# One hand-written schedule of a decoder layer replaced by another: orders, engines, PSUM banks, one VectorE branch and a three-row bias load

## The chip, the cores and the metric

The kernel runs on one core of one Trainium2 chip. The metric is the device time of one launch, in microseconds (us). Engines are called as in the profile: PE (TensorE), PEld (its weight loads), DVE (VectorE), ACT (ScalarE), POOL (GpSimd), SP (SyncE, which here only starts DMAs).

## The reference

```python
x = _layernorm(x + _L0_attn_ref(x, Wq, bq, Wk, bk, Wv, bv, Wo, bo, q_gain))   # 16 heads, 4 key heads, rms norm, rope, causal
x = _layernorm(x + _wkv(time_decay, time_first, k=x, v=ctx_2048))            # a decaying scan over 128 steps, divided
x = _layernorm(x + down(relu(up(x) * up_scale)) * down_scale * output_scale)  # weights are signs, 256 -> 1024 -> 256
```

x and ctx_2048 are 16 x 128 x 256 in float32.

## The kernel before

The 16 sequences are worked on in eight pairs, p = 0 to 7 (T = 2 sequences of 128 rows a pair). Every pair passes through three stages. Attention: `project` (PE), `squares` and `take_values` (ACT), `rope_sines`, `rope_cosines`, `rope_sum` and `head_sums` (DVE), `mean_log` and `first_root` (ACT), `newton_rms` (DVE, four small steps), `scale_heads`, `high_heads`, `low_heads`, `swap_keys` (these build `stack`, float16 high and low parts), a transposing DMA into `rows` (pair 0 by PE in `first_rows`, copied by `first_rows_out`), `scores`, `exps`, `products`, `project_out`, `residual`. Context: `keys`, `keys_by_context`, `scan`, `mix`, `log_den`, `first_rec`, `den_by_rec`, `num_by_rec`, `refine`, `add_mixed`. FFN: `high_x2`, `low_x2`, then for four quarters n `ffn_up`, `relu`, `high_bits`, `low_bits`, `ffn_down`, and at the end `scale_out` and `add_out`. Each stage ends in a layer norm: `moments` (DVE), `inverse_root` and `root` (GpSimd), then `normed` on DVE, or `offsets` on DVE and `normed` on ACT.

No compiler orders the work. Each engine has a list of calls, written out in full, in which the pairs are interleaved, and the engines meet at semaphores. `done(eng, name, p)` waits for a step of pair p. The table `ON` says by one letter a pair on which engine a step runs (V, G, A for DVE, GpSimd, ACT). The tables `PJ`, `SC`, `PV`, `AC`, `WO`, `X1`, `YT`, `X2`, `DN` and `UP` give the PSUM bank (of eight) of each product. Where two users share a bank, the later waits for the reader of the earlier. `hidden(p, n)` is in SBUF for n = 2 and in a PSUM bank otherwise.

Large gains need a row maximum ahead of the exps (`row_scores` on PE, `row_maxima` on DVE). Whether they do is known at run time: DVE writes two flags. PE loads one after project(1) and branches once, with two copies of everything that follows. DVE loads the other after head_sums(2) and has eight small branches, one a pair:

```python
guarded = dve.value_load(flags[0:1, 1:2], min_val=0, max_val=1)
with dve.If(guarded):
    row_maxima(0)
```

The biases are loaded to 96 partitions and split into three bfloat16 parts at rows 0, 32 and 64, which a product with `ones_b` adds up.

Of the kernel before, what the change touches and what calls it, by code (L numbers as in the profile page):

```python
# [22 lines left out]
T = 2  # L23
# [7 lines left out]
BR = 96  # L31
# [12 lines left out]
def build(nc, x, xT, ctxT, wqkv, biases, gains, wo, decay_in, first_in, up, down, up_s, down_s, out_s,  # L44
          rope_cos, rope_sin, ident_in, out):
    with ExitStack() as ctx:
# [3 lines left out]
        def sem(name):  # L50
# [26 lines left out]
        OUT_N = 2  # L77

# [16 lines left out]
        flags = sb("flags", [128, 2], I32)  # L95
# [62 lines left out]
        x2hi = sb("x2hi", [128, NC, T, S], F16)  # L158
        x2lo = sb("x2lo", [128, NC, T, S], F16)
# [14 lines left out]
        spare = probs[0:BR, 2].rearrange("p g j s -> p (g j s)")  # L174
        bias_in = spare[:, 0:E + D]
        bias_rest = spare[:, E + D:2 * (E + D)]
# [13 lines left out]
            o3_done=1, r3_done=1, ag3=1, ve3=1, rs3=1, out_done=2, of1=2, of2=2, of3=2, msq_done=1, vy3_done=1)  # L190
# [14 lines left out]
        PJ = (0, 2, 4, 0, 2, 0, 6, 2)  # L205
        SC = (((2, 6), (2, 4)), ((0, 4), (2, 4)), ((6, 4), (0, 4)), ((2, 4), (6, 4)),
              ((0, 4), (0, 4)), ((4, 2), (2, 4)), ((6, 4), (6, 2)), ((2, 0), (4, 6)))
        PV = ((6, 7), (2, 3), (0, 1), (6, 7), (0, 1), (2, 3), (2, 3), (0, 1))
        AC = (6, 2, 0, 7, 0, 0, 5, 6)
        WO = (6, 2, 1, 6, 4, 4, 3, 3)  # L210
        X1 = (3, 6, 6, 6, 4, 2, 6, 5)
        YT = (0, 7, 0, 5, 3, 5, 3, 5)
        X2 = (7, 5, 6, 2, 7, 3, 7, 0)
        DN = (1, 4, 5, 6, 0, 1, 4, 6)
        UP = ((7, 6, 1, 0), (6, 5, 4, 7), (6, 2, 3, 4), (2, 4, 3, 3),
              (7, 2, 0, 1), (4, 7, 5, 6), (4, 7, 5, 6), (7, 5, 1, 7))


        IN_SBUF = ((0, 0, 1, 0), (0, 0, 1, 0), (0, 0, 1, 0), (0, 0, 1, 0),
                   (0, 0, 1, 0), (0, 0, 1, 0), (0, 0, 1, 0), (0, 0, 1, 0))  # L220
        LAST_IN_PSUM = (0, 0, 0, 0, 0, 0, 0, 1)

        WHOLE = ()
        FIRST = 2
# [4 lines left out]
        slots = dict(xT_in=XT_N, x_in=X_N, ctx_in=CTX_N, rows_in=ROWS_N, stored=OUT_N)  # L229
# [8 lines left out]
        bias_out_in = sem("bias_out_in")  # L238
# [29 lines left out]
        def done(eng, name, p, k=None):  # L268

            k = names[name] if k is None else k  # L270
            before = ON[name][:p].count(ON[name][p]) if name in ON else p
            eng.wait_ge(signal(name, p), before * names[name] + k)

        def turn(name, p):

            return p - 1 if name in ("rows_in", "xT_in") else p
# [9 lines left out]
        def hidden(p, n):  # L286

            if n in WHOLE:
                return hid[:, p % HID_N]
            if IN_SBUF[p][n]:  # L290
                return hid[:, sum(IN_SBUF[q][n] for q in range(p)) % HID_N]
            return banks[:, UP[p][n]].rearrange("p (j s) -> p j s", j=2)

        def down_of(j):

            return dn_f[:, j] if j // 2 in WHOLE else dn_sb[:, j]

        def scaled(p):

            return banks[:, DN[p]].rearrange("p (t d) -> p t d", t=T) if LAST_IN_PSUM[p] else r3[:, p % R3_N]  # L300

# [10 lines left out]
        GAINS = 7  # L312
# [8 lines left out]
        def _(sp):  # L321
# [25 lines left out]
            sp.dma_start(bias_in[:, 0:E], biases[0:E].partition_broadcast(BR)).then_inc(bias_in_done, 16)  # L347
# [13 lines left out]
            load_xT(4)  # L361
            load_x(0)
            head_rows(1)
            load_x(1)
            load_xT(5)
            load_xT(6)
# [1715 lines left out]
```

## Time and the profile before

| | |
|---|---|
| median of 3 runs | 178.62 us (178.32 to 179.33) |
| span of the profiled execution | 178.1 us (no separate time of that execution was recorded) |
| busy PE, DVE, ACT, POOL | 157.8, 156.5, 138.9, 83.4 us |
| granted TensorE clock, mean | 0.979 |
| read from and written to HBM | 9.52 and 2.10 MB |

The profile is that of one execution. Busy time is the time in which an engine had an instruction in work; neighbours overlap a little. The idle time that a row shows in brackets is the one ahead of it, with what ended it; "issue" is time for which the profile has no releaser.

### The profile page before, as it was taken

How to read it: one execution, taken by the hardware profiler on the slowest of the kernel's cores; microseconds unless marked ns; L12 is line 12 of the kernel's file. 1: busy time of each engine (PE TensorE's matmuls, PEld its weight loads, DVE VectorE, ACT ScalarE, POOL GpSimd, SP SyncE). 2: the span in 40 equal slices, each digit the busy share in tenths (PEclk: the TensorE clock that was granted, in tenths of full speed). 3: DMA queues.
4: the chain of work that ended last, by engine and by line, in shares of the span. 5: the costliest groups of instructions: out<-in, count | busy, mean ns of one | idle time of the engine just before them, and what ended most of it. 6: DMA issues, size and time to landing. Idle time of an engine off the chain costs nothing.

```text
span 178.1 us, 3837 instructions
## 1 busy us (share of the span) xinstructions
PE 157.8 (89%) x1388; PEld 107.8 (61%) x1388; DVE 156.5 (88%) x289; ACT 138.9 (78%) x280; POOL 83.4 (47%) x109
## 2 busy tenths in 40 slices
PE   7978769989999999999999999999969798999920
PEld 2445424545645645566886668769758687898810
DVE  1489679798789999999899999999999999999981
ACT  3745488988998889999899989696687897898700
POOL 8282601017404695020873623699679457270121
PEclk9999969999999999999999999999999999999995
DMA  5899039044709107941070310000300010001122
GB/s 175 244 320 392 5 62 209 2 92 75 249 0 95 56 2 94 212 127 48 0 151 0 75 48 2 0 4 0 118 0 4 0 59 0 36 27 61 63 79 107
DMA packets 17989, 14.65 MB, mean 82 GB/s; under 512 B 12656, under 2 KB 13616, under 8 KB 17712
## 3 DMA queue, kind: packets, MB, share of 16 engines
q1 hardware_dynamic: 17424, 13.87, 29.8%
q10 hardware_dynamic: 544, 0.50, 0.9%
q8 instruction: 13, 0.21, 0.5%
q14 instruction: 8, 0.07, 0.1%
HBM read 9.52 MB, written 2.10 MB: 65 GB/s over the span
## 4 chain that ended last, share of the span: by engine, by line
PE 48%; DVE 27%; ACT 10%; issue 8%; DMA 3%; POOL 2%; SPq 0%; POOLq 0%; DVEq 0%; ACTq 0%
PE banks L417 9%; PE banks L576 8%; PE banks L500 7%; PE banks L597 6%; PE banks L533 5%; DVE hid_lo L1760 5%; DVE state L1702 4%; PE banks L472 4%; ACT probs L971 3%; DMA probs<-biases_dram 3%; DVE ratio L1712 2%; DVE stats L1676 2%; PE banks L510 2%; ACT dn_sb L918 2%; PE banks L479 2%
## 5 line engine op out<-in xcount | busy, mean ns | idle before, releaser
L971 ACT ACTIVATE probs<-banks 128x1024 f32<-128x1024 f32 x32 | 31.8, 1022 | 4.8 <-PE banks L479 4.8
L597 PE MATMUL banks<-dn_sb,hid_hi 128*128 128x256 bf16 x128 | 29.1, 272 | 1.1 <-DVE hid_lo L1760 1.1
L576 PE MATMUL banks<-x2hi,up_sb 128*128 128x256 f16 x128 | 29.1, 273 | 0.8 <-DVE x2lo L1753 0.5
L597 PE MATMUL banks<-dn_sb,hid_lo 128*128 128x256 bf16 x128 | 29.1, 273 | 0.0
L576 PE MATMUL banks<-x2lo,up_sb 128*128 128x256 f16 x128 | 29.0, 272 | 0.0
L417 PE MATMUL banks<-wqkv_sb,xT_sb 128*128 128x384 f32 x64 | 23.5, 512 | 2.0 <-issue 1.6
L1355 POOL TENSOR_SCALAR veps<-stats 128x2 f32<-128x2 f32 x24 | 9.4, 394 | 27.8 <-DVE stats L1676 26.8
L1361 POOL TENSOR_TENSOR rstd<-veps,half_neg 128x2 f32<-128x2 f32 x24 | 20.4, 853 | 1.3
L1019 ACT ACTIVATE banks<-banks,ups_man 128x256 f32<-128x256 f32 x48 | 19.6, 470 | 1.8 <-PE banks L576 1.6
L417 PEld LDWEIGHTS banks<-wqkv_sb,xT_sb 128*128 128x128 f32 x64 | 12.4, 201 | 11.9 <-issue 3.4
L1702 DVE TENSOR_TENSOR_SCAN state<-dec_sb,ke 128x1032 f32<-128x1032 f32 x8 | 18.4, 2301 | 0.0
L500 PE MATMUL banks<-probs,v_sb 128*32 128x512 f32 x128 | 17.6, 632 | 0.2
L576 PEld LDWEIGHTS banks<-x2hi,up_sb 128*128 128x128 f16 x128 | 12.5, 98 | 6.0 <-issue 3.8
L1760 DVE TENSOR_TENSOR hid_lo<-banks,hid_hi 128x512 f16<-128x512 f32 x24 | 16.0, 679 | 0.0
L1025 ACT ACTIVATE hid_hi<-banks 128x512 f16<-128x512 f32 x24 | 14.3, 616 | 1.7 <-PE banks L597 0.8
L533 PE MATMUL banks<-wo_sb,attT_sb 128*128 128x256 f32 x64 | 15.1, 379 | 0.0
L597 PEld LDWEIGHTS banks<-dn_sb,hid_hi 128*128 128x128 f16 x128 | 12.5, 98 | 3.4 <-issue 1.8
L597 PEld LDWEIGHTS banks<-dn_sb,hid_lo 128*128 128x128 f16 x128 | 12.5, 98 | 1.5
L576 PEld LDWEIGHTS banks<-x2lo,up_sb 128*128 128x128 f16 x128 | 12.5, 98 | 1.4
L533 PEld LDWEIGHTS banks<-wo_sb,attT_sb 128*128 128x128 f32 x64 | 12.2, 190 | 1.5
L472 PE MATMUL banks<-rows 32*128 32x512 f16 x128 | 10.2, 394 | 3.2 <-ACT probs L971 1.5
L1405 POOL TENSOR_TENSOR hid_lo<-hid,hid_hi 128x512 f16<-128x512 f32 x5 | 5.8, 1168 | 14.7 <-ACT hid_hi L1025 14.6
(129 smaller groups left out, 355.8 us busy)
## 6 DMA issues: line engine op xcount, KB each, us to landing
ctxT_sb<-ctxT_dram SPq DMA_DIRECT2D x8, 256.0 KB, 3.1
x_sb<-x_dram SPq DMA_DIRECT2D x8, 256.0 KB, 3.8
out_dram<-outb SPq DMA_DIRECT2D x8, 256.0 KB, 2.2
xT_sb<-xT_dram SPq DMA_DIRECT2D x7, 256.0 KB, 4.4
up_f<-up_dram SPq DMA_DIRECT2D x1, 1024.0 KB, 6.4
dn_f<-down_dram SPq DMA_DIRECT2D x1, 1024.0 KB, 8.4
wqkv_sb<-wqkv_dram ACTq DMA_DIRECT2D x2, 192.0 KB, 3.1
xT_sb<-xT_dram SPq DMA_DIRECT2D x2, 128.0 KB, 2.9
```

Of the source, the lines that this page charges most:

```text
L417: nc.tensor.matmul(banks[:, b + t, 0:E], xT_sb[:, p % XT_N, c, t, :], wqkv_sb[:, c, :], start=(c == 0), stop=False)
L472: nc.tensor.matmul(banks[:, b[g]], q[r:r + VW, kb, :], q[r:r + VW, HB * t:HB * t + REP, :].rearrange("p j s -> p (j s)"), start=(k == 0), ...
L500: nc.tensor.matmul(banks[r:r + VW, PV[p][t], :], v_sb[:, p % V_N, t, g, :], probs[:, (T * p + t) % PROBS_N, g].rearrange("p j s -> p (j s) ...
L533: mm = nc.tensor.matmul(banks[:, WO[p], t * D:(t + 1) * D], attT_sb[:, c, t, :], wo_sb[:, c, :], start=False, stop=(t == T - 1 and c == NC ...
L576: mm = nc.tensor.matmul(banks[:, UP[p][n], s * T * S:(s + 1) * T * S], up_sb[:, c, j * 128:(j + 1) * 128], part[:, c, :, :].rearrange("p t ...
L597: mm = nc.tensor.matmul(banks[:, DN[p], t * D:(t + 1) * D], part[:, t * S:(t + 1) * S], down_of(j), start=(j == 0 and t == 0 and m == 0), ...
L971: nc.scalar.activation(probs[:, (T * p + t) % PROBS_N, 2 * h:2 * h + 2].rearrange("p n j s -> p n (j s)"), banks[:, b:b + 2], ACT.Exp).the ...
L1019: nc.scalar.activation(hidden(p, n)[:, s], banks[:, UP[p][n], s * T * S:(s + 1) * T * S], ACT.Relu, scale=ups_man[:, j:j + 1]).then_inc(se ...
L1025: nc.scalar.activation(hid_hi[:, 2 * n:2 * n + 2], hidden(p, n), ACT.Copy)\
L1361: nc.gpsimd.tensor_tensor(rstd[n][:, p % MV_N], veps[n][:, p % MV_N], half_neg[:], ALU.pow)\
L1702: nc.vector.tensor_tensor_scan(state[:, 1:2 * W + 1], dec_sb[:].rearrange("p c a t s -> p (c a t s)"), ke[:, p % KE_N].rearrange("p c a t ...
L1760: nc.vector.tensor_tensor(hid_lo[:, 2 * n:2 * n + 2], hidden(p, n), hid_hi[:, 2 * n:2 * n + 2], ALU.subtract).then_inc(signal(f"lo{n}_done ...
```

## The change

No arithmetic of the layer changes. The lists of all five engines and all bank tables are written anew. `ON` has more rows and new letters: `high_bits` is on GpSimd seven times (before never), `low_bits` eight times (before five), `add_out` never (before three times), `swap_keys` on DVE five times (before once). The third norm is on ACT for five pairs, the first for five, the second for six (before 0, 0 and 8). PE runs project(2), project(3) and first_rows ahead of its branch. DVE has one branch ahead of the first rope step, with two copies of what follows. One DMA of three rows replaces both bias loads, behind a memset of the 96 rows; the output bias is split on DVE instead of GpSimd; the gains are loaded by SP instead of ACT. x2 has its high and low part in one tile `x2T` of two slots. The last pair's FFN output is handled in halves. `X2_BY_DMA` is 0 for all pairs, so its paths are not taken.

```diff
-        spare = probs[0:BR, 2].rearrange("p g j s -> p (g j s)")
-        bias_in = spare[:, 0:E + D]
+        bias_in = outb[0:BR].rearrange("p n t d -> p (n t d)")[:, 0:E + D]
+        bias_rest = r3[0:BR].rearrange("p n t d -> p (n t d)")[:, 0:E + D]
-            qn_done="GGVVGGGV",
-            hi_done="AGGGGAGA",
-            lo_done="VGVVGGGG",
-            stack_done="AVAAAAAA",
-            kv_done="VGVVGVGG",
-            newt_done="GGGVGGVG",
-            lo2_done="GGGVGGVV",
-            r3_done="GGVGVVVV")
+            hi0_done="GAAGAAAA",
+            hi1_done="AGAAAAAA",
+            hi2_done="AGAAAGAA",
+            hi3_done="AAGAAAAG",
+            hi_done="GGGGGGAA",
+            kv_done="VVGVVVGG",
+            lo1_done="VVGVVVGV",
+            lo2_done="GVGVVVVV",
+            lo3_done="VVGVGGGV",
+            lo_done="GGGVGVGG",
+            newt_done="VGGGGGGV",
+            out_done="AAAVVAAV",
+            qn_done="VGGGVGGV",
+            stack_done="VAVVAVAV",
+            x1_done="VAAVAAAV",
+            x2_done="VAAAAAAV")
-        IN_SBUF = ((0, 0, 1, 0), (0, 0, 1, 0), ...
+        HID = ((1, -1, 1, -1), (-1, 0, 1, -1), (-1, 1, 0, 0), (1, -1, -1, -1), (-1, -1, -1, 0), (-1, 1, 0, 1), (-1, 0, -1, 1), (0, 1, -1, 0))
...
-            sp.dma_start(bias_in[:, 0:E], biases[0:E].partition_broadcast(BR)).then_inc(bias_in_done, 16)
+            sp.wait_ge(bias_clear, 1)
+            sp.dma_start(bias_in[0:BR:32], biases.partition_broadcast(3)).then_inc(bias_in_done, 16)
+            for dst, src in gain_loads:
+                sp.dma_start(dst, src).then_inc(gains_in, 16)
...
             project(0)
             project(1)
-            pe.wait_ge(masks_ready, MASKS)
-            pe.wait_ge(guard_ready, GUARDS)
+            project(2)
+            done(pe, "rot_done", 0)
+            project(3)
+            first_rows()
             pe.wait_ge(gain_ready, GAINS)
             plain = pe.value_load(flags[0:1, 0:1], min_val=0, max_val=1)
...
                 scores(0, 0, guarded)
                 done(pe, "probs_done", 0, 1)
                 done(pe, "rot_done", 2)
                 scores(0, 1, guarded)
+                done(pe, "probs_done", 0, 2)
+                project(4)
+                done(pe, "probs_done", 0, 3)
                 products(0, 0)
-                done(pe, "probs_done", 0, 3)
-                project(4)
+                products(0, 1)
                 done(pe, "rot_done", 3)
...
-                ffn_down(7, 3)
+                ffn_down_half(7, 0)
+                ffn_down_half(7, 1)
...
+            def scale_half(p, t):
+
+                done(dve, "dn_mm", p, NJ // 2 + t)
+                nc.vector.tensor_tensor(down_tile(p, t), down_tile(p, t), dsc_b[:], ALU.mult).then_inc(sems["o3_done"], 1)
+
+            def add_half(p, t):
+
+                done(dve, "o3_done", p, t + 1)
+                nc.vector.tensor_tensor(r3[:, p % R3_N, t], down_tile(p, t), x2[:, p % X2_N, t], ALU.add)\
+                    .then_inc(signal("r3_done", p), 1)
...
+            nc.vector.memset(bias_in, 0.0).then_inc(bias_clear, 1)
             split_biases()
             gains_constants()
+            dve.wait_ge(gain_ready, GAINS)
+            plain = dve.value_load(flags[0:1, 0:1], min_val=0, max_val=1)
+
+            def from_heads(guarded):
+
+                rope_sines(0)
+                rope_cosines(0)
+                head_sums(0)
+                rope_sum(0)
+                newton_rms(0)
+                scale_heads(0)
+                rope_sines(1)
+                head_sums(1)
+                rope_cosines(1)
+                swap_keys(0)
...
+                low_bits(7, 2)
+                low_bits(7, 3)
+                add_out(6)
+                moments(2, 6)
+                scale_half(7, 0)
+                done(dve, "out_done", 5)
+                add_half(7, 0)
+                scale_half(7, 1)
+                add_half(7, 1)
+                offsets(2, 6)
+                moments(2, 7)
+                landed(dve, "stored", 5)
+                normed(2, 7)
+
+            with dve.If(plain):
+                from_heads(False)
+            with dve.Else():
+                from_heads(True)
```

## Rows read from the trace of the kernel before

**Rows 1.** The page's first part: busy us, share of the span, instructions
```profile
PE 157.8 (89%) x1388; PEld 107.8 (61%) x1388; DVE 156.5 (88%) x289; ACT 138.9 (78%) x280; POOL 83.4 (47%) x109
```
**Rows 2.** Windows: length, busy PE, PEld, DVE, ACT, POOL, clock, DMA share, GB/s
```profile
50.00:110.00 60.00, 58.10 (x589) 37.74 (x588) 57.85 (x91) 54.87 (x105) 27.22 (x31) 1.00 0.35 67
110.00:152.00 42.00, 38.14 (x334) 31.30 (x332) 41.84 (x69) 33.59 (x72) 29.61 (x29) 1.00 0.06 20
152.00:170.50 18.50, 18.20 (x166) 15.81 (x163) 17.29 (x34) 14.79 (x33) 4.79 (x9) 1.00 0.12 45
```
**Rows 3.** Timeline of DVE and PE, 6 to 11 us: start, length, instruction
```profile
6.95 0.35 DVE L1518 CAST bias_rows<-probs 96x384 bf16<-96x384 f32 x1 [5.30 <-DMA probs<-biases_dram]
...
8.92 0.50 PE L423 MATMUL banks<-bias_rows,ones_b 96*128 96x384 bf16 x2 [0.35 <-DVE bias_rows L1524]
...
10.19 0.82 DVE L1575 TENSOR_REDUCE ssum<-sq 128x40 f32<-128x640 f32 x1 [0.35 <-ACT sq L923]
```
**Rows 4.** DMA issues: KB each, median us from issue to landing
```profile
xT_sb<-xT_dram SPq DMA_DIRECT2D x2, 128.0 KB, 2.9
...
gain_in<-gains_dram ACTq DMA_DIRECT2D x1, 8.0 KB, 5.5
```
**Rows 5.** Timeline of PE, 13 to 31 us
```profile
13.92 2.84 PE L417 MATMUL banks<-wqkv_sb,xT_sb 128*128 128x384 f32 x8 [1.59 <-issue]
...
19.83 0.83 PE L431 MATMUL banks<-id_h,stack 128*128 128x128 f16 x12
21.78 0.61 PE L472 MATMUL banks<-rows 32*128 32x512 f16 x8 [1.12 <-ACT rows L964]
...
24.10 1.04 PE L472 MATMUL banks<-rows 32*128 32x512 f16 x8 [1.48 <-ACT probs L971]
...
30.50 0.61 PE L472 MATMUL banks<-rows 32*128 32x512 f16 x8
```
**Rows 6.** Timeline of POOL, the last guard table
```profile
12.20 0.61 POOL L1338 CAST maskq_sb<-probs 128x512 bf16<-128x512 f32 x1
```
**Rows 7.** Groups by line and shape: busy us, mean ns, idle before
```profile
L1381 POOL TENSOR_TENSOR stack<-qn,stack 128x640 f16<-128x640 f32 x5 | 7.0, 1402 | 0.4 <-ACT stack L948 0.2
...
L1612 DVE TENSOR_TENSOR banks<-banks,cos_sb 128x640 f32<-128x640 f32 x8 | 6.6, 830 | 0.6 <-issue 0.4
...
L1374 POOL CAST stack<-qn 128x640 f16<-128x640 f32 x5 | 3.6, 717 | 15.1 <-DVE qn L1635 14.9
...
L1584 DVE SCALAR_TENSOR_TENSOR vy<-ssum,ysq 128x40 f32<-128x40 f32 x8 | 1.6, 200 | 0.3
```
**Rows 8.** Timeline of DVE at its first branch and pair 2
```profile
22.30 0.83 DVE L1612 TENSOR_TENSOR banks<-banks,cos_sb 128x640 f32<-128x640 f32 x1 [0.45 <-issue]
23.17 0.82 DVE L1619 TENSOR_TENSOR rot<-banks,rope_b 128x640 f32<-128x640 f32 x1
```
**Rows 9.** Windows of one us: the last but two is the clock
```profile
26.00:27.00 1.00, 1.00 (x8) 0.00 (x0) 0.15 (x1) 1.00 (x3) 0.00 (x0) 0.50 2.29 185
```
**Rows 10.** Groups by line and shape, of norms, low halves and products
```profile
L1760 DVE TENSOR_TENSOR hid_lo<-banks,hid_hi 128x512 f16<-128x512 f32 x24 | 16.0, 679 | 0.0
...
L1035 ACT ACTIVATE x<-z,offset,rstd 128x256 f32<-128x256 f32 x16 | 8.8, 613 | 1.3 <-DVE offset L1682 1.2
...
L1691 DVE TENSOR_SCALAR outb<-r,stats,rstd 128x256 f32<-128x256 f32 x16 | 5.8, 404 | 1.2 <-POOL rstd L1361 1.2
...
L1734 DVE TENSOR_TENSOR ratio<-ratio,rec 128x512 f32<-128x512 f32 x5 | 4.7, 932 | 0.0
```
**Rows 11.** Timeline of DVE and POOL where both work in SBUF
```profile
59.57 1.73 DVE L1734 TENSOR_TENSOR ratio<-ratio,rec 128x512 f32<-128x512 f32 x1
...
134.23 2.68 POOL L1361 TENSOR_TENSOR rstd<-veps,half_neg 128x2 f32<-128x2 f32 x1
```
**Rows 12.** Timeline of PE and DVE, the end
```profile
170.18 0.27 PE L597 MATMUL banks<-dn_sb,hid_lo 128*128 128x256 bf16 x1
...
174.47 0.73 DVE L1691 TENSOR_SCALAR outb<-r,stats,rstd 128x256 f32<-128x256 f32 x2 [1.23 <-POOL rstd L1361]
```

More of the change, by code:

```diff
@@ L286, in hidden, with x2_part, down_tile @@
         def hidden(p, n):
[L288 to L291, printed above, removed]
+            if HID[p][n] >= 0:
+                return hid[:, HID[p][n]]
             return banks[:, UP[p][n]].rearrange("p (j s) -> p j s", j=2)
[L294 to L300, printed above, removed]
+        def x2_part(p, part):
+            return x2T[:, p % X2T_N, part].rearrange("p t c s -> p (t c s)")
+        def down_tile(p, t):
+            if p == PAIRS - 1:
+                return banks[:, DN[p] + t, 0:D]
+            return banks[:, DN[p], t * D:(t + 1) * D]
         def alone(eng):
@@ L401, in _ @@
             store(7)
-            for p in range(PAIRS - OUT_N, PAIRS):
-                landed(sp, "stored", p)
+            landed(sp, "stored", PAIRS - 3)
+            landed(sp, "stored", PAIRS - 2)
+            landed(sp, "stored", PAIRS - 1)
         @block.tensor
@@ L1469, in _ @@
             root(1, 3)
-            inverse_root(2, 0)
-            inverse_root(2, 1)
+            root(2, 0)
             low_bits(2, 2)
             inverse_root(0, 6)
-            root(2, 0)
             root(0, 6)
-            root(2, 1)
+            inverse_root(2, 1)
+            high_bits(2, 3)
+            low_bits(2, 3)
             inverse_root(1, 4)
@@ L1500, in _ @@
             root(2, 4)
+            low_bits(6, 3)
             inverse_root(2, 5)
             root(2, 5)
+            high_bits(7, 3)
             inverse_root(2, 6)
@@ L1863, in _ @@
-            offsets(1, 0)
-            rope_cosines(7)
-            rope_sum(7)
-            scan(1)
-            with dve.If(guarded):
-                row_maxima(5)
-            residual(3)
-            mix(1)
-            low_x2(0)
-            newton_rms(7)
-            keys_by_context(2)
-            attend_norm(4)
-            moments(0, 3)
-            num_by_rec(1)
-            scale_heads(7)
-            scan(2)
-            refine(1)
-            low_bits(0, 0)
-            done(dve, "ny_done", 1)
@@ L1901, in _ @@
-            done(dve, "x1_done", 3)
-            residual(5)
-            with dve.If(guarded):
-                row_maxima(7)
-            low_x2(1)
-            keys_by_context(3)
-            offsets(1, 2)
-            scan(3)
-            moments(0, 5)
-            moments(2, 0)
-            mix(3)
-            low_bits(1, 0)
-            done(dve, "ratio_done", 3)
-            scan(4)
-            low_x2(2)
-            attend_norm(6)
-            low_bits(1, 1)
-            den_by_rec(3)
@@ L1919, in _ @@
-            refine(3)
-            low_bits(1, 3)
-            low_bits(2, 0)
-            done(dve, "ny_done", 3)
-            mix(4)
-            scale_out(1)
-            add_mixed(3)
-            moments(1, 3)
-            residual(6)
-            low_bits(2, 1)
-            normed(0, 5)
-            moments(0, 6)
-            moments(2, 1)
-            refine(4)
-            keys_by_context(5)
-            offsets(1, 3)
-            scan(5)
-            attend_norm(7)
-            low_bits(2, 3)
```

1048 lines of the change are left out of this document (528 added, 520 removed).

## The prediction

> **What bounds the kernel now.** I read the busy shares first [rows 1]: PE 157.8 and DVE 156.5 of 178.1 us. Two engines share the load, so a price counts only in the stretch where its engine ends last. The windows [rows 2] split that: from 50 to 110 us PE is busy 58.10 and DVE 57.85 of 60; from 110 to 152 DVE is full (41.84 of 42) while PE has 3.9 us of holes; from 152 to 170.5 PE is full (18.20 of 18.5). Then come 7.6 us in which PE does nothing. So I look for three things: PE's holes before 31 us, DVE's load after 110, and the tail.
>
> **The start, before.** DVE waits 5.30 us for the 96-row bias load, and PE's bias product starts 0.35 late for it [rows 3]. PE's next hole, 1.59, carries the label "issue" [rows 5], but its branch waits for the guard tables too, and GpSimd ends the last of them at 12.81 [rows 6]. So the branch itself is some 1.1 (13.92 - 12.81). PE stands again 1.12 for the copy of the first rows, and 1.48 before scores(0,1) [rows 5]: labelled with the first exps, but rotation 2, for which the order also waits, ends at 23.99 [rows 8], 0.11 before the matmul. After these holes the granted clock is half (0.50, 1.2 GHz) between 24 and 27 [rows 9].
>
> **The start, after, step by step.** The three-row load is asked of SP behind a clearing memset on DVE. No row has that memset; it lies between nothing and the 0.83 of a 128x640 pass [rows 7], and SP asks for the bias no earlier than 1.65 anyway (5.30 before 6.95 [rows 3]). Landing: between the 2.9 of the first xT halves and the 5.5 of the gains [rows 4]. With the split (1.9: 6.95 to about 8.9 [rows 3]) the bias is there between 6.5 and 9.1; project(0)'s own matmuls end at 8.57. I take no wait: PE 0.35 earlier. GpSimd's four out-bias steps (8.97 to 11.3) go to DVE later on, four more of some 0.3 to 0.5 each, about 1.3 in all.
>
> PE now runs project(2), project(3) and the first transposes before its branch: from 8.57, the bias product (0.33) and three projections of about 2.9 end at 17.6 if nothing holds them (before: 19.83 [rows 5]). What can hold them is the stack of pair 0. DVE starts on squares(0) at about 10.0 (before 10.19 [rows 3]; 0.35 earlier, and 0.27 later as the values are taken first). Sines, cosines, row sums, rotation sum and scale_heads (now on DVE), each at the row's 0.83 or a little under, and four small steps of 0.20 with their gaps, 0.87: 14.95 [rows 7]. GpSimd's copy 0.72 and subtraction 1.40 [rows 7] end at 17.25, and DVE's two small copies at 17.6. So stack and PE meet at 17.6. Transposes end at 18.5, ACT's copy at 19.5, and PE's branch (1.1) at 19.6, inside the copy. scores(0,0) starts at 19.6 to 19.9 instead of 21.78: 1.9 to 2.2 gained, all of it branch, guard tables and bias.
>
> DVE then does sines, cosines and sum of pair 2 straight after the rows: 22.1 instead of 23.99, so scores(0,1) keeps the gain. project(4) follows, then both products. At 28.4 scores(1,0) could start, with rotation 3 ready at 28.4 also (two head sums and the small constants, 1.1, are ahead of it). Before it started at 30.50 [rows 5] with products(0,1), 1.0 us, still to do. That is 3.1 ahead. But PE has a hole of about 1.5 at 20.7 again, and by the row at half clock 3 us of work cost 1.3 more here too; then it is 1.7. I take 2.0 for the whole start, ends 0.8 (stack or branch late) and 3.1.
>
> The one large branch on DVE replaces eight small ones. These cost little: 0.45 idle at the first [rows 8], which holds the value load, and nothing to see at the others. The new one costs 0.45 to 1.1 and stands before the first sines. It is hidden under the wait for squares(0) until 10.0, if the gains, now third in SP's queue, land by 7.6; if they and the branch are late it is 1.2 on the path that feeds the stack.
>
> **The late stretch.** I counted DVE's calls from mix(4) to the end. Gone: six norm pairs net (11 to 5; x 0.64 at the pace of the row's 404 ns each, overlapped) = -3.8, three low_bits (x 0.60) = -1.8. Added: two add_out and one moments (x 0.61) = +1.8, six offsets (x 0.1, half of the 0.20 of a small step [rows 7], as they overlap) = +0.6. Net -3.2 us [rows 10]. ACT gets seven norms and loses one (x 1.05 a pair [rows 10]: +6.3), and four high_bits go to GpSimd (-2.1): ACT, with 33.6 of 42 busy from 110 to 152 [rows 2], goes to some nine tenths. GpSimd has holes enough. DVE is the full engine there and PE has 3.9 of holes, so up to 3.2 comes back; dependence on longer GpSimd and ACT chains keeps part of it. The middle of 0 and 3.2 leans up because nothing else is full: I take 1.8. The two-slot x2T removes ACT's waits on up_mm before high_x2; ACT is not the last there, so nothing for it. The x2T operand is read in two runs of 128 instead of one of 256, the same columns: no cost, as the out-bias product reads its operand in two runs already, at the pace of the scores' of the same width.
>
> **Two engines at one SBUF.** GpSimd's 0.69 us root of a 128x2 tile took 2.68 while a scan ran, and a DVE product 1.73 while GpSimd's began just before it [rows 11]; the five such products have a mean of 0.93 [rows 10], undisturbed ones take 0.67. So each can block the other. GpSimd gets seven high_bits and three more low_bits (about 1.2 each), and loses three add_out. Those five carry an excess of 1.3 us in all, the most of what DVE lost beside some thirty long GpSimd steps; ten more cost some 0.6 by that, inside the 1.8; the worst, each blocking for 1.06, is the slower rival below.
>
> The Trainium skill (SBUF — State Buffer, "Who interferes with whom") says that a VectorE instruction with two SBUF inputs and a GpSimd instruction that reads SBUF exclude each other for the whole instruction, by order of issue. The trace agrees in both directions [rows 11]. By it low_bits from a PSUM bank would not collide, while those whose hidden half is in SBUF (16 of 32 now, 8 before) and all add_out would; if each of these eight more collided at the 1.06 above, 8.5 us would be the bill instead of 0.6.
>
> **The tail.** Before, PE's last matmul starts at 170.18, DVE's last norm ends at 175.20 [rows 12], 4.75 after PE, and the store takes the rest. After, norm(2,6) is on ACT (0.65 off DVE), and the last out tile comes in halves: scale 0 overlaps PE's last four matmuls, then three half steps of about 0.4 stand where two of 0.69 stood, with one offset of 0.1 ahead of the last moments. From PE's end: 1.4, moments 2.1, GpSimd 3.3, norm 4.1. Gain 0.6 (0.3 to 0.9).
>
> **Sum.** 2.0 + 1.8 + 0.6 = 4.4. The profiled execution's span is 178.1, and its own time is not given, so I carry the difference to the median: 178.62 - 4.4 = 174.2.
>
> **The rivals.**
> - Late relief lost: DVE gets lighter, but ACT or the GpSimd chains set PE's waits, and only start and tail stay: 178.6 - 2.6 = 176.0. For it: ACT's +4.2 in that stretch. Against: its 8.4 us of holes.
> - Everything at its upper end, 3.1 + 3.2 + 0.7: 171.6. For it: all three holes are of known cause. Against: two engines at 96% in the middle.
> - The change doesn't do what it says: the stack or DVE's branch is late by 1.2, the clock falls longer, and the middle, where PE has 1.9 of holes in 60, eats the rest: 178.3.
> - Slower, by blocking: GpSimd's added SBUF readers stand ahead of scans and refines. It decides once DVE's excess passes 5.0 (the sum of 4.4 and the 0.6 already in it), that is when five of the ten block for 1.06. With seven of them, 7.4 us, of which 0.7 reaches the end (42 of the 60 us after 110 have a full DVE), and no late gain: 178.6 - 2.6 + 5.2 = 181.2.
>
> **Chances.** Forecast (172.6 to 175.6) 0.45, late relief lost 0.20, upper end 0.13, no gain 0.08, slower 0.14. The range goes from 171.6, the upper end, to 178.4, the no-gain case; the forecast's own stands above. A measurement tells 0.5% (0.9 us) from no change. Faster 0.78, within 0.08, slower 0.14.
>
> **What would show it.** scores(0,0) on PE at 19.6 to 19.9, no 1.59 hole at 12, and DVE's branch gap ending before 10.2. scores(1,0) between 27.5 and 29. From mix(4) on DVE less by 3 us, PE's holes there under 2.5, ACT near nine tenths. Last norm 4.1 after the last matmul. The forecast is wrong if the three-row load lands after 7.2, if GpSimd's stack of pair 0 is later than 17.6, if the half clock lasts over 3 us, or if DVE's two-input steps have a mean over 0.75.

## The result, and the profile after

The changed kernel takes 176.33 us (median of 4 runs, 176.1 to 176.81), the kernel before beside it 178.86 (4 runs, 178.32 to 179.33): a ratio of 0.987, with a 95% interval of 0.983 to 0.991. The forecast was 174.2 in a range of 171.6 to 178.4. The sign and the range held; the gain is 2.5 us, where 4.4 was forecast. The profiled execution has a span of 174.3 and a time of 176.1.

The first part of the page of the changed kernel answers to [rows 1]: busy us, share of the span, instructions. Below it are windows of the same trace, which answer to [rows 2]:

```profile
PE 155.2 (89%) x1388; PEld 107.4 (62%) x1388; DVE 157.6 (90%) x295; ACT 140.7 (81%) x280; POOL 83.8 (48%) x113
```
```profile
50.00:110.00 60.00, 56.69 (x570) 38.89 (x567) 58.19 (x95) 52.92 (x102) 26.69 (x31) 1.00 0.28 67
110.00:152.00 42.00, 39.33 (x346) 32.00 (x346) 41.50 (x69) 37.87 (x82) 27.70 (x34) 1.00 0.08 26
```

From 110 to 152 ACT has 37.87 of 42, the forecast nine tenths, and PE's holes are 2.67 in place of 3.86. But from 50 to 110 PE stands 3.3 us where it stood 1.9.

PE's timeline of the start, which answers to [rows 5] (the projections in it have no hole between them):

```profile
17.10 0.84 PE L441 MATMUL banks<-id_h,stack 128*128 128x128 f16 x12
19.06 0.61 PE L488 MATMUL banks<-rows 32*128 32x512 f16 x8 [1.12 <-ACT rows L972]
...
21.53 0.61 PE L488 MATMUL banks<-rows 32*128 32x512 f16 x8 [1.64 <-ACT probs L979]
...
27.41 0.61 PE L488 MATMUL banks<-rows 32*128 32x512 f16 x8
```

DVE's timeline there, which answers to [rows 3]:

```profile
4.64 0.56 DVE L1503 CAST bias_rows<-outb 96x384 bf16<-96x384 f32 x1 [2.32 <-DMA outb<-biases_dram]
...
7.36 0.15 DVE L1534 TENSOR_SCALAR flags<-small_f 128x1 int32<-128x1 f32 x1
9.54 0.89 DVE L1594 TENSOR_TENSOR rope_b<-banks,sin_sb 128x320 f32<-128x320 f32 x2 [2.02 <-ACT sq L931]
```

The three bias rows are there at 4.6 and their split ends at 6.8, at the early end of the forecast 6.5 to 9.1. The flags are ready at 7.5, and DVE's branch lies inside the wait for the squares until 9.54. scores(0,0) starts at 19.06 (forecast 19.6 to 19.9, in the kernel before 21.78) and scores(1,0) at 27.41, just before the forecast 27.5 to 29. The clock stays at 1.00 from 20 to 28.

Two places lose time. The timeline of DVE and POOL of the changed kernel at 100 us, with PE's instruction that waits:

```profile
99.37 2.17 POOL L1389 CAST hid_hi<-hid 128x512 f16<-128x512 f32 x2 [7.89 <-ACT hid L1032]
...
101.51 1.27 POOL L1384 TENSOR_TENSOR ratio<-ratio,rec 128x512 f32<-128x512 f32 x1
101.69 3.30 DVE L1752 TENSOR_TENSOR hid_lo<-hid,hid_hi 128x512 f16<-128x512 f32 x2
102.74 1.71 POOL L1379 TENSOR_TENSOR newt<-ratio,rec 128x512 f32<-128x512 f32 x1
...
105.14 0.27 PE L614 MATMUL banks<-dn_sb,hid_hi 128*128 128x256 bf16 x1 [1.56 <-DVE hid_lo L1752]
```

Two low halves take 3.30 us. When nothing disturbs them it is 1.27 (an experiment below has them so). And at 162 us, where offsets(2,5) stands ahead of scale_out(6) and two low halves on DVE:

```profile
162.28 1.10 POOL L1345 TENSOR_TENSOR rstd<-veps,half_neg 128x2 f32<-128x2 f32 x1
...
163.49 0.60 DVE L1671 SCALAR_TENSOR_TENSOR offset<-stats,rstd 128x2 f32<-128x2 f32 x1 [0.65 <-POOL rstd L1345]
...
165.43 0.27 PE L614 MATMUL banks<-dn_sb,hid_hi 128*128 128x256 bf16 x1 [1.22 <-DVE hid_lo L1752]
```

DVE stands 0.65 for GpSimd's root, the offset itself takes 0.60 instead of 0.15, and PE's 1.22 is its only hole after 150. The groups of the low halves by where the hidden half lies (mean ns of one), against the 679 of [rows 10]:

```profile
L1752 DVE TENSOR_TENSOR hid_lo<-banks,hid_hi 128x512 f16<-128x512 f32 x15 | 9.9, 679 | 0.7 <-ACT hid_hi L1038 0.5
L1752 DVE TENSOR_TENSOR hid_lo<-hid,hid_hi 128x512 f16<-128x512 f32 x9 | 8.1, 907 | 0.3 <-ACT hid_hi L1038 0.3
```

The fifteen that read a PSUM bank keep 679; the nine that read two SBUF tiles have a mean of 907, though their median is 684: the two at 101.69 carry the excess. The Trainium skill (SBUF — State Buffer, "Who interferes with whom") says that a VectorE instruction with two SBUF inputs contends with a GpSimd instruction that reads SBUF, and one with at most one SBUF input, outside VectorE's 2-port modes, does not. The trace agrees (907 against 679), and adds that only those pay which meet such a GpSimd instruction in time.

### The profile page after: what moved, and what is told of

The parts are those of the page before. It is cut to its first block, busy times and chain, and to the rows that moved or that the text cites. A ratio compares the mean times of both kernels' runs of the same rounds, so it can differ in the third digit from the quotient of the medians.

```text
span 174.3 us, 3825 instructions
## 1 busy us (share of the span) xinstructions
PE 155.2 (89%) x1388; PEld 107.4 (62%) x1388; DVE 157.6 (90%) x295; ACT 140.7 (81%) x280; POOL 83.8 (48%) x113
## 4 chain that ended last, share of the span: by engine, by line
DVE 38%; PE 36%; ACT 11%; issue 8%; POOL 4%; POOLq 0%; DVEq 0%
DVE state L1691 8%; PE banks L427 7%; PE banks L614 7%; PE banks L593 5%; DVE hid_lo L1752 5%; PE banks L549 4%; ACT probs L979 3%; DVE stats L1665 3%; DVE ratio L1701 3%; PE banks L516 2%; DVE rot L1608 2%; PE banks L632 2%; DVE rope_b L1594 2%; POOL stack L1365 2%; PE banks L488 2%
## 5 line engine op out<-in xcount | busy, mean ns | idle before, releaser
L593 PE MATMUL banks<-x2T,up_sb 128*128 128x256 f16 x256 | 32.5, 273 | 0.7 <-DVE x2T L1747 0.5
L593 PEld LDWEIGHTS banks<-x2T,up_sb 128*128 128x128 f16 x256 | 24.1, 98 | 6.7 <-DVE x2T L1747 1.2
L1339 POOL TENSOR_SCALAR veps<-stats 128x2 f32<-128x2 f32 x24 | 6.2, 258 | 28.3 <-DVE stats L1665 27.2
L1345 POOL TENSOR_TENSOR rstd<-veps,half_neg 128x2 f32<-128x2 f32 x24 | 18.4, 768 | 1.5
L1032 ACT ACTIVATE hid<-banks,ups_man 128x256 f32<-128x256 f32 x34 | 14.4, 483 | 1.6 <-DVE hid_lo L1752 0.8
L1394 POOL TENSOR_TENSOR hid_lo<-hid,hid_hi 128x512 f16<-128x512 f32 x8 | 10.0, 1246 | 7.3 <-ACT hid_hi L1038 7.2
L1032 ACT ACTIVATE banks<-banks,ups_man 128x256 f32<-128x256 f32 x30 | 12.3, 458 | 1.3 <-PE banks L593 1.3
L1379 POOL TENSOR_TENSOR newt<-ratio,rec 128x512 f32<-128x512 f32 x6 | 8.9, 1483 | 7.9 <-ACT rec L1012 7.8
L1701 DVE SCALAR_TENSOR_TENSOR ratio<-ke,now_gain,state 128x512 f32<-128x512 f32 x16 | 12.0, 794 | 0.1
L1389 POOL CAST hid_hi<-hid 128x512 f16<-128x512 f32 x7 | 6.5, 933 | 10.3 <-ACT hid L1032 10.2
```

The lines of the kernel that those rows point to most:

```text
L593: mm = nc.tensor.matmul(banks[:, UP[p][n], s * T * S:(s + 1) * T * S] .rearrange("p (t s) -> p t s", t=T), up_sb[:, c, j * 128:(j + 1) * 1 ...
L1032: nc.scalar.activation(hidden(p, n)[:, s], banks[:, UP[p][n], s * T * S:(s + 1) * T * S], ACT.Relu, scale=ups_man[:, j:j + 1]).then_inc(se ...
L1345: nc.gpsimd.tensor_tensor(rstd[n][:, p % MV_N], veps[n][:, p % MV_N], half_neg[:], ALU.pow)\
L1394: nc.gpsimd.tensor_tensor(hid_lo[:, 2 * n:2 * n + 2], hidden(p, n), hid_hi[:, 2 * n:2 * n + 2], ALU.subtract).then_inc(signal(f"lo{n}_done ...
L1701: nc.vector.scalar_tensor_tensor(ratio[:, c].rearrange("p a t s -> p (a t) s"), ke[:, p % KE_N, c].rearrange("p a t s -> p (a t) s")[:, :, ...
```

## The experiments

There are eighteen runs; three kernels came twice, and one run is the kernel before by itself. A ratio is to the kernel before on the same chip, with its 95% interval. Executions of one kernel differ by PE's mean clock over the run, so I also give the mean of those at 0.985 or above ("at the higher clock"), where that tells more. "Up to the last norm" means: to the end of DVE's last instruction in the profiled execution.

**The kernel before, again.** No edit.

> The kernel before once more, for a second profiled execution. Theory A (its time depends on whether TensorE's clock falls to half after the holes at 20 to 24 us): if its mean clock is 0.985 or above, the windows from 24 to 28 us show 1.00 and the span is 176 to 176.8; if it is 0.982 or below, they show 0.5 to 0.6 and the span is 177.3 or more. Theory B (the clock is not what tells its executions apart): a span of 177.3 or more with the clock at 1.00 from 24 to 28 us, or below 176.8 with a fall there.

Measured: 178.73 (12 runs), ratio 1.001 [0.998, 1.004]; profiled at a mean clock of 0.987 with a span of 176.4, 1.7 below the first profile. PE's timeline and the windows of this execution:

```profile
13.52 2.84 PE L417 MATMUL banks<-wqkv_sb,xT_sb 128*128 128x384 f32 x8 [1.78 <-issue]
...
21.38 0.61 PE L472 MATMUL banks<-rows 32*128 32x512 f16 x8 [1.12 <-ACT rows L964]
23.70 0.61 PE L472 MATMUL banks<-rows 32*128 32x512 f16 x8 [1.48 <-ACT probs L971]
```
```profile
50.00:110.00 60.00, 58.19 (x596) 38.23 (x589) 57.91 (x93) 54.80 (x107) 27.25 (x31) 1.00 0.33 67
```

The holes of 1.12 and 1.48 are those of [rows 5], the first is 1.78 for 1.59, the clock stays at 1.00 from 20 to 30, and from the first scan on no stretch differs by more than 0.05 from the first profile. Theory A held. Over all these runs the kernel before had 48 executions at 0.985 or above (mean 178.3) and 53 below (mean 179.8); one more of 404 us is left out. The profile that I predicted from was one of the longer kind: a run's time is 1.7 to 1.9 above its span, but for the two kernels named below (1.4 to 1.6), which makes it an estimated 179.9, 1.0 above the median of 178.86. Not all of its distance to the second profile is the clock: it is 0.40 later at scores(0,0) already (21.78 for 21.38), ahead of the fall, and 1.67 later at scores(1,0) behind it (30.50 for 28.83), so the fall costs 1.27.

**The changed kernel, twice more.** No edit.

> The changed kernel once more, on the same chip as the other three, as their reference. Both theories: 0.985 to 0.989 of the kernel before, 2.0 to 2.7 us less. It also shows whether the profiled span of before, 178.1 us, is typical: the changed kernel's time is its span and 1.8 us, so if before has the same 1.8 its spans should be some 177.0.

> The changed kernel once more, beside the two others. By theory A it is 175.7 to 176.4, the same as the kernel before with only the branch moved; by theory B 1 us or more below that one.

Measured: 175.73, ratio 0.982 [0.977, 0.986], and 176.29, ratio 0.984 [0.979, 0.990]. Of its 16 executions one was below 0.985. By the mean of all executions the change is worth 3.0 (179.13 to 176.16); by executions of the higher clock alone 2.2 (178.34 to 176.12).

**PE's branch alone, in the kernel before.**

```diff
             project(1)
+            project(2)
+            done(pe, "rot_done", 0)
+            project(3)
+            done(pe, "rot_done", 1)
+            first_rows()
             pe.wait_ge(masks_ready, MASKS)
...
-                project(2)
-                done(pe, "rot_done", 0)
-                project(3)
-                done(pe, "rot_done", 1)
-                first_rows()
```

> The kernel before with one part of the change: PE runs project(2), project(3) and first_rows ahead of its branch. Theory A (the 1.59 us ahead of project(2) were guard tables and branch, and the branch hides under the copy of the first rows): the hole at 12 us is gone, scores(0,0) starts at 20.2 to 21.0 instead of 21.78, limited by the stack of pair 0 (18.4 us), and 0.5 to 1.4 us of it reach the end. Theory B (VectorE's rotation of pair 2 sets scores(0,1), so the lead is lost at 24 us): under 0.4 us at the end.

> The kernel before with TensorE's branch alone moved behind the first rows, a second time, now beside the changed kernel on the same chip. Theory A (that place is nearly the whole gain): within 0.4 us of the changed kernel, 0.985 to 0.99 of the kernel before, its granted clock at 0.985 or above in all executions. Theory B: the changed kernel is ahead of it by 1 us or more, as the late stretch was worth something.

Measured: 176.39, ratio 0.988 [0.984, 0.993], all six at 0.985 or above; the second time 177.32, ratio 0.989 [0.984, 0.994], with five of twelve below. At the higher clock it is 176.4 and 176.7, so 1.6 to 1.7 below before, and 0.4 above the changed kernel beside it. In its trace the hole at 12 is gone and scores(0,0) starts at 19.68, earlier than the 20.2 to 21.0 expected, and more reaches the end than the 1.4 that was the upper end of theory A. The expectation that its clock never falls did not hold the second time, so by the medians the changed kernel is 1.0 ahead of it there, and neither theory settles it by itself: 0.4 is left at the higher clock, the rest is the clock.

**PE's branch set back, in the changed kernel.** The diff is the reverse of the one above, in the changed kernel, with the waits for the guard tables and masks again.

> The changed kernel whole, but for TensorE's branch, which stands after project(1) again with its waits for the guard tables and masks. Theory A (the place of that branch is nearly the whole gain; the new orders, banks, engine choices, the bias load and the single VectorE branch together are worth little by the end): TensorE has a hole of about 1.5 us at 12 to 13 us, holes before scores(0,0) and scores(0,1), the granted clock falls to half for some us in part of the executions, scores(1,0) starts at 29.5 to 30.5, and the median is 178.0 to 179.5, within 0.5% of the kernel before. Theory B (the new orders carry a gain of their own of 1.5 us or more, and the branch only adds to it): 176.8 to 177.5, with the lead over before growing after 110 us.

Measured: 176.24, ratio 0.984 [0.979, 0.990]. Theory A, that the place of this branch is nearly the whole gain, fell, and the time lies below the 176.8 of theory B too. PE's timeline:

```profile
11.15 0.49 PE L433 MATMUL banks<-bias_rows,ones_b 96*128 96x384 bf16 x2
11.48 2.74 PE L427 MATMUL banks<-wqkv_sb,xT_sb 128*128 128x384 f32 x8
```

No hole at all: the branch costs nothing between two projections when what it waits for is there. GpSimd's last table ends at 8.7 now, as its four bias steps went to DVE and the identity matrix lands 1.3 earlier; before it ended at 12.81 [rows 6]. The 1.1 that I called the price of the branch is real, but it counts from the end of the last wait and runs beside the matmuls that are queued. From the end of GpSimd's last table to the start of project(2) are 1.11 and 1.13 in the two profiles before, and 1.10 in both profiles of the start set back, below. In one of these the tables end (11.29) 0.31 ahead of the queued matmuls, and the hole is 0.79.

**The guard tables early, in the kernel before.**

```diff
             half_identity()
-            split_out_biases()
             guard_tables()
+            split_out_biases()
```

> The kernel before, with GpSimd's four out-bias steps behind the guard tables instead of ahead of them, and nothing else; TensorE's branch stands where it stood. Theory A (the hole of 1.59 at 12 us is the wait for the guard tables, and the branch has a price only where such a wait ends just ahead of it): the tables end at about 10.7, TensorE's hole at 12 is gone or below 0.3, scores(0,0) starts about 1.5 earlier and the median is 176.2 to 177.4, that of the kernel with only the branch moved. Theory B (the branch costs TensorE 1.1 wherever it stands between projections): a hole of 1.1 stays at 12 us, and the median is 178.0 to 179.5.

Measured: 177.18, ratio 0.992 [0.988, 0.995]; at the higher clock 176.9, 1.4 below before. Theory A held: the tables end at 10.44 and PE has no hole at 12 (project(2) follows at 12.32 with the branch ahead of it). One moved line gives over half of the change's gain. In its profiled execution the first scan is only 0.7 ahead of before, as the bias came late and PE waited 1.75 for it.

**The changed kernel with its start set back.**

```diff
-            sp.dma_start(bias_in[0:BR:32], biases.partition_broadcast(3)).then_inc(bias_in_done, 16)
+            sp.dma_start(bias_in, biases.partition_broadcast(BR)).then_inc(bias_in_done, 16)
...
             half_identity()
+            split_out_biases()
             guard_tables()
```

and PE's branch behind project(1); in the second of the two GpSimd's bias steps also wait for DVE's split.

> The changed kernel with its start set back in three points: TensorE's branch after project(1), the bias load with 96 rows, and the out-bias steps on GpSimd ahead of the guard tables. Theory A (nearly all of the gain is the start, by either of two sufficient edits): TensorE's hole at 12 us is back with 1.0 to 1.6, and the median is 177.7 to 179.2. Theory B (the late stretch is worth 1 us or more by itself): 176.3 to 177.5, and the lead over before grows between 110 and 160 us.

> As start_undone, but GpSimd's out-bias steps wait for VectorE's split of the first bias, so that the guard tables end at 11.8 to 12.6. Theory A (the rest of the change is worth nothing by the end; all of the gain is the start): TensorE's hole at 12 us is 1.3 to 2.0, the first scan starts at 47.8 to 49.2, and time up to the last norm's end is that of the kernel before within 0.7 us. Theory B (the rest is worth 1 us or more): it is 1 us or more earlier there. The 1.9 us behind the last norm: if they come again, they belong to this program; if not, to that execution.

Measured: 178.98, ratio 1.003 [0.999, 1.006], with a hole of 0.79 (one of its twelve executions took 321 us and is left out), and 178.86, ratio 1.004 [1.000, 1.007], with a hole of 1.61. By time theory A of the first held. But these times don't say what they seem to. Both spans go on for 4.6 to 4.8 us behind DVE's last norm, where all the others take 2.5 to 3.0, and no engine works in what they have more. It came in both, so it belongs to the program. From 165 us on both traces show four packets on one of the queues of instruction loads, where the changed kernel has two or three; whether they are the cause was not tried. Up to the last norm the second of them is 1.0 us ahead of before:

```profile
12.56 2.84 PE L427 MATMUL banks<-wqkv_sb,xT_sb 128*128 128x384 f32 x8 [1.61 <-issue]
```
```profile
47.29 2.31 DVE L1702 TENSOR_TENSOR_SCAN state<-dec_sb,ke 128x1032 f32<-128x1032 f32 x1
...
171.88 0.73 DVE L1691 TENSOR_SCALAR outb<-r,stats,rstd 128x256 f32<-128x256 f32 x2 [1.23 <-POOL rstd L1359]
```

The same two in the kernel before, again:

```profile
49.07 2.31 DVE L1702 TENSOR_TENSOR_SCAN state<-dec_sb,ke 128x1032 f32<-128x1032 f32 x1
...
172.86 0.73 DVE L1691 TENSOR_SCALAR outb<-r,stats,rstd 128x256 f32<-128x256 f32 x2 [1.23 <-POOL rstd L1361]
```

So it is 1.8 ahead at the first scan and 1.0 at the end, outside the 0.7 of theory A of the second. In this pair the new order of the first 45 us is worth 1.8 even with the hole, and what follows loses 0.8 of it.

**The 96-row bias load alone, in the changed kernel.** The first of the two edits above.

> The changed kernel with its one bias load to all 96 rows instead of three. Theory A (the broadcast is what lands late; 5.3 us before): the bias product starts after 8.6 us, the time is 0.2 to 1.5 us more, since the gains stand behind it in SP's queue too. Theory B (the load is hidden behind the first projection either way): within 0.2 us.

Measured: 177.52 (12 runs), ratio 0.991 [0.986, 0.995], six of twelve below 0.985. At the higher clock it is 176.6, 0.3 to 0.7 above the two versions beside it (176.3 and 175.9). The bias product starts at 7.71, 0.23 late, and not after 8.6 as theory A had it, though the time is in its range. In its profile the stack is 0.65 late for the first rows, and the clock is 0.50 from 22 to 25.

**Eight branches on DVE, and the last tile whole.** The first has `dve.If(guarded)` around each row maximum again and no large branch; the second takes ffn_down(7, 3), scale_out(7) and add_out(7) in place of the halves.

> The changed kernel with eight small branches on VectorE again (a second flag, and one branch around each row maximum) instead of one large branch; the value load stays where it is. Theory A (a small branch that is not taken costs next to nothing, and the large one is hidden under the wait for the first squares): within 0.4 us of the changed kernel. Theory B (each branch stops VectorE's look-ahead for some 0.1 to 0.4 us, and VectorE is full): 0.8 to 3 us more.

> The changed kernel with the last pair's output as one tile again (one product group, one scale_out, one add_out). Theory A, by the steps as counted: two full steps of 0.69 stand where three half steps of 0.42 and the wait for the last product stood, so 0.3 to 0.5 us more. Theory B (the halves' handshakes eat what they save): within 0.15 us.

Measured: 176.33, ratio 0.989 [0.984, 0.994], and 176.23, ratio 0.986 [0.979, 0.993]. Neither edit is worth what can be measured. The changed kernel itself did not run on their chip, but the traces say the same: from the start of the first scan to the end of the last norm they take 125.32 and 125.29 us, the changed kernel 125.31, 125.34 and 125.35. Theory A held for the branches, theory B for the tile.

**offsets(2,5) later.**

```diff
                 low_bits(7, 1)
-                offsets(2, 5)
+                done(dve, "out_done", 4)
                 scale_out(6)
                 low_bits(7, 2)
                 low_bits(7, 3)
+                offsets(2, 5)
```

> One call of VectorE moved: offsets(2,5), which waits for GpSimd's root, from ahead of scale_out(6) and low_bits(7,2), low_bits(7,3) to behind them. Theory A (the lead of 4.6 us at low_x2(7) falls to 2.5 at the last product because VectorE stands at this call, while PE waits 1.22 us for low_bits(7,2)): 0.6 to 1.2 us less than the changed kernel, and no PE hole over 0.3 us after 160 us. Theory B (PE would wait there for ACT's or GpSimd's high half of quarter 3 anyway): less than 0.3 us, with the hole moved to the last quarter.

Measured: 175.63, ratio 0.982 [0.977, 0.987], three of six below 0.985; at the higher clock 175.0, against 175.9 of the changed kernel beside it. From the second part of x2(7) to DVE's end it takes 14.5 us, as before did (14.5), the changed kernel 15.5, and PE has no hole left after 150. Theory A held.

**The high halves of pair 1 on ACT, alone and with the offsets later.**

```diff
-            hi1_done="AGAAAAAA",
-            hi2_done="AGAAAGAA",
+            hi1_done="AAAAAAAA",
+            hi2_done="AAAAAGAA",
```

> high_bits(1,1) and high_bits(1,2) are on ACT again, as in the kernel before; nothing else is changed. Theory A (GpSimd is busy in SBUF without a break from 99.4 to 104.5 us and keeps VectorE's two low halves of quarters 1 and 2, which ran 3.30 us for 1.28, and the lead over before falls by 2.2 us there): the two run in 1.3 to 1.5 us, PE's hole of 1.56 us at 105 shrinks under 0.6, and the time falls by 1.0 to 2.0 us. Theory B (the lead falls there because the first FFN quarters compete with attention for ACT, and blocking only fills time that VectorE would wait): within 0.4 us of the changed kernel or slower, as ACT gets 1.2 us more.

> Both edits together. Theory A, the two losses are separate and add up: 1.6 to 3.0 us less than the changed kernel, 172.8 to 174.6. Theory B: nothing outside 0.5 us.

Measured: 176.58, ratio 0.986 [0.981, 0.991], and with the offsets 175.29, ratio 0.979 [0.975, 0.984], 0.4 below the changed kernel beside it where theory A had 1.6 to 3.0. The first theory fell: without GpSimd's high halves the low halves are as slow, and the trace shows the two products of pair 3 beside them.

```profile
101.68 1.27 POOL L1386 TENSOR_TENSOR ratio<-ratio,rec 128x512 f32<-128x512 f32 x1 [10.13 <-ACT rec L1012]
101.77 3.40 DVE L1752 TENSOR_TENSOR hid_lo<-hid,hid_hi 128x512 f16<-128x512 f32 x2
102.91 1.71 POOL L1381 TENSOR_TENSOR newt<-ratio,rec 128x512 f32<-128x512 f32 x1
```

**The two products of pair 3 on DVE, alone and with the offsets later.**

```diff
-            guess_done="VVVGGVGV",
+            guess_done="VVVVGVGV",
-            newt_done="VGGGGGGV",
+            newt_done="VGGVGGGV",
...
-            num_by_rec(3)
-            den_by_rec(3)
...
                 low_bits(1, 3)
+                den_by_rec(3)
+                num_by_rec(3)
                 refine(3)
```

> The changed kernel with num_by_rec(3) and den_by_rec(3) on VectorE, alone. Theory A (their blocking of the two low halves reaches the end): 175.2 to 175.6, 0.5 to 1.0 below the changed kernel. Theory B (the time won at 105 us is lost again by the end, and the gain of the version with both edits came from offsets(2,5)): 175.7 to 176.4, the same as the changed kernel.

> The changed kernel with num_by_rec(3) and den_by_rec(3) moved from GpSimd to VectorE, just ahead of refine(3), and offsets(2,5) behind low_bits(7,3). Theory A (these two GpSimd steps are what blocked the two low halves of pair 1, 3.30 us in place of 1.28): the two low halves take 1.3 to 1.4, VectorE reaches refine(3) 0.6 to 0.8 earlier than in the changed kernel even with 1.3 of steps more, TensorE's hole of 1.56 at 105 us shrinks below 0.5, and the median is 174.3 to 175.2. Theory B (the hole has another owner, or the two steps cost VectorE as much as the blocking did): refine(3) starts at 106.3 or later and the median is 175.0 to 175.8, that of the version with only offsets(2,5) moved.

> The changed kernel with num_by_rec(3) and den_by_rec(3) on VectorE and offsets(2,5) behind low_bits(7,3), once more. If both repairs hold: 174.2 to 175.2, at 0.974 to 0.980 of the kernel before; if the first time was luck, 175.5 or more.

Measured: alone 176.12, ratio 0.985 [0.982, 0.988]; with the offsets 174.58, ratio 0.976 [0.970, 0.982], and again 174.54, ratio 0.977 [0.972, 0.983]. The timeline of DVE and POOL of the version with both:

```profile
100.91 1.27 DVE L1750 TENSOR_TENSOR hid_lo<-hid,hid_hi 128x512 f16<-128x512 f32 x2
101.16 1.08 POOL L1339 TENSOR_SCALAR veps<-stats 128x2 f32<-128x2 f32 x1 [0.40 <-DVE stats L1663]
```

The low halves take 1.27, and DVE reaches the scan of pair 5 0.67 earlier in relation to the first scan, although it has two more products. PE's hole for the low halves at 105 is gone, but one of 1.70 stands at 106.68 for refine(3) in its place, where I had expected less than 0.5; refine(3) itself takes 1.45, beside a low half on GpSimd, and the mix behind it 1.42 instead of 2.19.

By its times the edit alone brings nothing: 176.0 at the higher clock, in three executions, and 175.9 for the changed kernel on that chip, as theory B had it. Its profiled execution had the clock at 0.50 for three us from 22, though nothing in the edit is there. The trace behind that says otherwise:

```profile
47.62 2.31 DVE L1689 TENSOR_TENSOR_SCAN state<-dec_sb,ke 128x1032 f32<-128x1032 f32 x1
...
103.05 1.28 DVE L1750 TENSOR_TENSOR hid_lo<-hid,hid_hi 128x512 f16<-128x512 f32 x2
...
171.60 0.73 DVE L1678 TENSOR_SCALAR outb<-r,stats,rstd 128x256 f32<-128x256 f32 x2 [1.24 <-POOL rstd L1345]
```

From the first scan on, executions of one schedule agree within 0.1 us, whatever happened ahead of it. So small edits can be read there (us, from start to start on DVE, the last to the end of the last norm; "x2(7)" is its second part):

| schedule (profiles) | scan(0) to scan(4) | to scan(5) | to x2(7) | to the end | all |
|---|---|---|---|---|---|
| before (5, with its variants of the start) | 52.4 to 52.5 | 15.3 | 42.2 | 14.5 | 124.5 |
| changed (3) | 52.0 | 17.5 | 40.3 | 15.5 | 125.3 |
| offsets later | 52.0 | 17.5 | 40.3 | 14.5 | 124.3 |
| products on DVE | 52.0 | 16.85 | 40.3 | 15.5 | 124.7 |
| both (2) | 52.0 | 16.85 | 40.3 | 14.5 | 123.7 |

The two edits add up: 0.6 and 1.0 alone, 1.65 together. What the products win (2.0 of blocking, less 1.3 for two products more on DVE) does reach the end. The times of the edit alone hide it, as the first scan of the changed start lies anywhere from 45.5 to 46.6 at the full clock. At the higher clock the version with both has 174.5, the changed kernel on the same chip 176.3. This is the best version.

## Why the prediction was right in sign and too large

The clean account compares executions whose clock never fell: the kernel before, again (span 176.4), and the changed kernel (174.3, and 174.1 the third time). The first scan and the last norm of the changed kernel:

```profile
46.27 2.31 DVE L1691 TENSOR_TENSOR_SCAN state<-dec_sb,ke 128x1032 f32<-128x1032 f32 x1
...
170.85 0.73 DVE L1680 TENSOR_SCALAR outb<-r,stats,rstd 128x256 f32<-128x256 f32 x2 [1.23 <-POOL rstd L1345]
```

Its lead on DVE, from where the same instruction starts:

| from | lead, us (third time) | forecast |
|---|---|---|
| scan(0), before at 49.07 | 2.8 (3.2) | start 2.0 |
| scan(4), before at 101.55 | 3.3 (3.7) | |
| scan(5), before at 116.87 | 1.1 (1.5) | |
| scan(7), before at 138.22 | 2.0 (2.4) | |
| second part of x2(7), before at 159.08 | 3.0 (3.4) | start and late 3.8 |
| DVE's end, before at 173.59 | 2.0 (2.4) | all 4.4 |

All of the gain is there at the first scan; what stands behind it, forecast at 2.4 more, takes 0.8 away. The orders differ, so a lead in the middle also says what was moved across that instruction.

- **The start (2.0, ends 0.8 and 3.1): under-sized.** It gave 2.8 to 3.2, its upper end. Each step was seen: no hole at 12, the bias early, DVE's branch hidden, scores(0,1) kept. I took off for half clock, and it did not fall. The working had one false item: the branch as a price of its own. Its 1.1 counts from the end of its last wait, so moving it and having the tables early do the same thing, and the change does both. (The 3.1 less the 1.3 of the clock is 1.8, not the 1.7 of the working.) Only one execution of before at the full clock has a trace, and nine of the changed start have the first scan at 45.5 to 46.6, so the gain is 2.4 to 3.6.
- **The late relief (1.8, ends 0 and 3.2): the step that failed.** Between the first scan and x2(7) the net is 0.2. The relief is there, 1.9 from scan(5) to x2(7). But 2.2 are lost just ahead of it, between scan(4) and scan(5), where the low halves of pair 1, with the hidden half in SBUF, meet GpSimd's two products of pair 3 (2.0), and the mix behind them stands beside a low half on GpSimd (0.8: 2.19 for 1.40; read from the trace, with no run of its own). With the two products on DVE the 2.0 is gone, which shows the cause. I had priced ten more collisions at 0.6, from the mean over all of before's, and counted DVE's instructions only from mix(4) on. The excess of DVE's two-input steps over their usual durations is 4.2 us in the changed kernel (2.0, 1.0, 0.8 and 0.5 in four places, the 1.0 and the 0.5 on small steps) and 1.5 before (1.1, 0.3, 0.2): 2.7 more, below the 5.0 from which I let it decide. The bill of 8.5, had each low half with two SBUF inputs collided, was too large in turn: nine low halves with two SBUF inputs are on DVE and eight on GpSimd (17 of 32, not 16), and two of the nine were blocked. The rival "slower, by blocking" named the mechanism, and the rival "late relief lost" (176.0) the outcome, for another reason: of PE's holes over 1 us after 100 only one, 1.08 at 112.35, is for ACT, and a norm that was moved there ends it.
- **The tail (0.6): it became a loss of 1.0, the second step that failed.** From the end of PE's last matmul to that of the last norm are 4.24 us (167.34 to 171.58; forecast 4.1, before 4.75), so that part gave 0.5. The halves are not its cause, as the whole tile has 4.23. But 1.5 are lost ahead of PE's end. I had priced an offset at 0.1 and not asked what is queued behind it: offsets(2,5) stands ahead of scale_out(6) and the last two low halves, waits for GpSimd's root, and PE waits 1.22 for what is behind it. Moved, the 1.0 comes back.
- **The baseline.** The sum was made against an execution of 178.1 span, an estimated 1.0 above the median in time, with half clock from 24 to 27. I carried it over as if the offset were nothing. The forecast had the clock's fall cost the same after as before; after, it came in one execution of 16.
- **The eight branches, the x2T slots and the bias passes on DVE** were costed at next to nothing, and the branches measured so; the other two were not tried alone.

The sum with the measured terms: 3.0 for the start, 0.2 for the late stretch, -1.0 for the tail is 2.2, which is the measured difference at the higher clock; the rest of the 3.0 by the mean is that the clock falls seldom after. What in the first 45 us gives the 1.8 that neither the branch nor the tables explain was not taken apart: project(4) ahead of the products and the earlier bias are candidates, the bias with 0.3.

## What to carry to other kernels

A VectorE instruction with both operands in SBUF is to be priced against the GpSimd instructions that stand beside it in the two orders, pair by pair, not by a mean: two such meetings took back what the moved instructions had won. A tiny instruction placed ahead of large ones costs the wait of its slowest input, so look up what is queued behind it. And before a sum is made against one profile, look whether that execution is a typical one: here it was 1.7 us later at the first scan than another execution of the same kernel, 1.27 of it by its clock. Where executions agree from some instruction on, as here from the first scan, read a late edit from there and not from the time of the whole.

## What was not expected of the hardware

- A value load with its branch on PE costs nothing between two runs of queued matmuls when its semaphores are already there (11.15 and 11.48 above, without a hole). Behind a wait that ends late the next matmul starts 1.10 to 1.13 after the end of the wait, in four traces.
- The same program has executions with half clock for some 3 us near 22 to 27 and ones without, with the same holes of 1.12 and 1.48 ahead in both. The mean times of executions below and above a mean clock of 0.985 differ by 1.5 us in the kernel before. The changed program does it seldom, but versions of it that differ only in the late stretch did it in half of theirs (three of six with the two products moved), so its holes at 20 us do not settle it; what does stays open.
- Two low halves of 0.64 each took 3.30 and 3.40 between two GpSimd products, of which the second took 1.71 for 1.27. A GpSimd scaling of a 128x2 tile took 1.08 beside two low halves, 0.19 elsewhere.
- A program with some GpSimd instructions more in its start had some 1.9 us more without work behind the last norm, in both of its versions; the cause is open.
